# Two-layer graph network on one core: wide one-hot products, a reordered front, and W's low part on GpSimd

## Chip, cores and metric

One core of one Trainium2 chip runs one launch. The metric is device microseconds of that core, the median of several executions; lower is better. Engines are called as in the profile: PE (TensorE matmuls), PEld (its weight loads), DVE (VectorE), ACT (ScalarE), POOL (GpSimd), SP (the queue that issues loads).

## What is computed

1250 nodes with 512 features, 21250 edges. Cut to what matters here:

```python
h = relu(layernorm(x))
hw = h @ W + b_w                          # 512 x 512
e = leaky_relu((hw @ a[:512])[dst] + (hw @ a[512:])[src] + b_a)
w = exp(e)
x = x + segment_sum(w / denom[dst] * hw[src], dst)
h = relu(layernorm(x))
x = x + experts(h, edges)                 # 4 experts of 2 SAGE layers, top 2
```

## The kernel before

The edges become a dense matrix of counts, `CT[s, d]` = how many edges go from node s to node d. Nodes stand in T = 10 tiles of 125, edges in 170 chunks of 125. Attention is then a dense product over tiles, and both expert layers use the counts too. Everything after the first 103 us (attention, mean aggregation, experts) is not touched by the change.

**Hot stage** (`hot_block`, `hot_columns`). PE makes, for 8 chunks at a time, the one-hot rows of the edges' sources: two products of 500 columns (L1811) of `e_q` (edge numbers, their squares and a row of ones) with `q_sel`. A chunk's value is 1 where the number fits and at most 0 elsewhere, so an eviction with a maximum against 0 gives the one-hots `onehot_p`. There are 22 blocks (the last holds 2 chunks) in three pairs of banks, so block u waits for the eviction of block u-3. ACT evicts 21 blocks (L794), DVE one (`HOT_DVE`, L1189). Into PE's sequence four small steps are written by hand at fixed places: `spread_spans` (L1818) and `turn_edges` (L1824) wait for DVE's edge numbers, `sum_tables` (L1830) and `turn_tables` (L1840) for DVE's table of which chunks each window of 25 nodes needs.

**Tiles** (`tile_and_batch`). For each of the 10 tiles PE turns the normalized rows `h_f` (L1898), makes 25 count products for 5 windows (L1860; DVE makes their other operand `onehot_g`, L1301, 25 instructions a tile), the attention scores (L1879, L1882: `hT` times `wa`, where `wa` = W times the vectors a, made once by DVE in `sources`, L1184 to L1266), and 12 products of 512 columns with W (L1923 to L1925). Float32 values are split in a high part (rounded, fp32r) and a low part, `hT_hi`/`hT_lo` and `W0_hi`/`W0_lo`; three of the four partial products are taken. ACT makes high parts (L770), DVE low ones (L1285 for hT, L1270 for W).

Each engine works through its own program in order; waits on semaphores are the only link. DVE's order at the front: edge numbers, `x_stats` (statistics of the rows of x, L1195) in gaps, the table (L1202 to L1236), the last five statistics and `x_mv` (L1242), then tile 0: 25 one-hots, `scales` (L1249), `sources`, `hT_lo`, `W0_lo`, and then tile 1's one-hots. ACT's order: `q_sel`'s second half (L778), the square (L788), 21 evictions with `e_gc`, `column` (L804, the window's numbers that DVE's one-hots need) and `std` between them, then `h_f` (L811), `W0_hi`, `hT_hi`. POOL makes constants up to 10.4 us and is then idle until the tiles end.

The stationary `e_q` and moving `q_sel` have 65 rows: 32 numbers, 32 squares, 1 row of ones:

```python
e_q = at("e_q", [2 * CR + 1, CG, P], F32R, 15040)          # CR = 32
q_sel = at("q_sel", [2 * CR + 1, CR, P], F32R, R1 + 20480)
link(g.memset(f32(e_q[2 * CR:, :, :]), 1.0))
```

Of the kernel before, what the change touches and what calls it, by code (L numbers as in the profile page):

```python
# [37 lines left out]
def gnn_kernel(nc, x, src, dst, W0, b_w, a_vec, b_a, gate_W, gate_b, Wl, bl, Wr, out):  # L38
# [3 lines left out]
    P = 125  # L42
# [34 lines left out]
    with ctx:  # L77
# [65 lines left out]
        e_q = at("e_q", [2 * CR + 1, CG, P], F32R, 15040)  # L143
# [6 lines left out]
        q_row = at("q_row", [2 * CR + 1, P], F32, 21920)  # L150
        q_at = at("q_at", [2 * CR + 1, CR], F32, 22432)
        q_sel = at("q_sel", [2 * CR + 1, CR, P], F32R, R1 + 20480)
# [327 lines left out]
        HOT_DVE = (2,)  # L480
# [125 lines left out]
        def _(pool):  # L606
# [14 lines left out]
            link(g.memset(q_at[2 * CR:, :], 1.0))  # L621
# [26 lines left out]
            g.memset(tab_b[:], 0).then_inc(consts.sem, 1)  # L648
            beyond = counts_beyond(pool)
# [116 lines left out]
        def _(act):  # L766
# [83 lines left out]
            act.wait_ge(*norm_ready(1))  # L850
            norm(0)
            act.wait_ge(*w0_in(16))
            copy(W0_hi[:], W0_f[:]).then_inc(w0_hi_ready.sem, 1)

            for b in range(T):
# [12 lines left out]
                bias_in(b)  # L868
# [269 lines left out]
        def _(dve):  # L1138
# [14 lines left out]
            v.memset(q_row[CR:2 * CR, :], -1.0)  # L1153
            link(v.tensor_tensor(q_f[2 * CR:, :], q_f[2 * CR:, :], q_f[2 * CR:, :], ALU.mult))
            link(v.tensor_scalar(q_row[2 * CR:, :], q_f[2 * CR:, :], -1.0, 1.0, ALU.mult, ALU.add))
            dve.sem_inc(row_made.sem, 1)
            dve.wait_ge(*q_consts(2))
            for k in range(2):
                c = slice(8 * k, 8 * k + 8)
                v.tensor_tensor(q_sel[:, c, :], q_row[:].unsqueeze(1).broadcast_to([2 * CR + 1, 8, P]),  # L1160
                                q_at[:, c].unsqueeze(2).broadcast_to([2 * CR + 1, 8, P]), ALU.mult
# [30 lines left out]

            def row_stats(tiles):
# [4 lines left out]
            dve.wait_ge(*x_in(32))  # L1198
            row_stats(range(0, 2))
# [19 lines left out]
            row_stats(range(2, 4))  # L1219
            dve.wait_ge(*n_summed(1))  # L1220
            v.tensor_copy(tab_f[:, 2:3], ps[0:NW, 7, 0:1]).then_inc(tab_f_ready.sem, 1)
            row_stats(range(4, T // 2))
# [30 lines left out]
            def sources():  # L1253
# [4 lines left out]
                for w in range(2):  # L1258
                    dve.wait_ge(*wa_f_ready(2 * KC - 1 + w))
                    v.scalar_tensor_tensor(spill[w][0:P, :], bw_b[:], 1.0, a_b[0:P, w, :], ALU.mult, ALU.mult,  # L1260
                                           accum_out=ab[:, w:w + 1]).then_inc(ab_ready.sem, 1)
                dve.wait_ge(*wa_f_ready(2 * KC))
                link(v.tensor_copy(wa[:, :, 0:2], wa_f[:]))
                v.tensor_tensor(wa[:, :, 2:4], wa_f[:], f32(wa[:, :, 0:2]), ALU.subtract).then_inc(wa_ready.sem, 1)
                dve.wait_ge(*ab_ready(2))
                v.tensor_scalar(s_add[:], ab[:, 0:1], ab[:, 1:2], ba_c[:], ALU.add, ALU.add).then_inc(wa_ready.sem, 1)  # L1266

            def first_weights_low():
                dve.wait_ge(*w0_hi_ready(1))
                v.tensor_tensor(W0_lo[:], W0_f[:], f32(W0_hi[:]), ALU.subtract).then_inc(w0_lo_ready.sem, 1)  # L1270
# [992 lines left out]
```

## Time and profile before

| | us |
|---|---|
| median of 3 runs | 745.5 (745.43 to 745.51) |
| the profiled execution | 744.08 |
| its span | 742.3 |
| PE busy in the span | 717.8 (97%) |
| DVE, ACT, POOL busy | 428.0, 398.1, 184.1 |

The span is the stretch between the first and the last instruction; the execution has 1.8 us around it. In the rows, a line with "xN" holds N instructions: the first number is the start of the first, the second the time from it to the end of the last. Brackets give idle time before it and what ended it. Matmuls overlap, so each one's own duration is longer than the distance between two starts.

### The profile page before, as it was taken

How to read it: one execution, taken by the hardware profiler on the slowest of the kernel's cores; microseconds unless marked ns; L12 is line 12 of the kernel's file. 1: busy time of each engine (PE TensorE's matmuls, PEld its weight loads, DVE VectorE, ACT ScalarE, POOL GpSimd, SP SyncE). 2: the span in 40 equal slices, each digit the busy share in tenths (PEclk: the TensorE clock that was granted, in tenths of full speed). 3: DMA queues.
4: the chain of work that ended last, by engine and by line, in shares of the span. 5: the costliest groups of instructions: out<-in, count | busy, mean ns of one | idle time of the engine just before them, and what ended most of it. 6: DMA issues, size and time to landing. Idle time of an engine off the chain costs nothing.

```text
span 742.3 us, 12047 instructions
## 1 busy us (share of the span) xinstructions
PE 717.8 (97%) x3574; PEld 582.2 (78%) x3574; DVE 428.0 (58%) x1056; ACT 398.1 (54%) x897; POOL 184.1 (25%) x204
## 2 busy tenths in 40 slices
PE   5899999999999999999999999999999999999994
PEld 3589977888888888777777777878888888888883
DVE  8899889999752538622722622657444544444341
ACT  6966769677653521511511511347677667767751
POOL 4000000000000100850300010045666555655511
PEclk9999999999999999999999999999999999999998
DMA  9100000111501247799699695379844994438950
GB/s 207 39 4 3 4 3 18 53 35 35 165 8 58 79 123 240 217 333 326 228 354 328 200 359 197 99 184 264 300 93 88 264 343 120 86 69 225 290 156 6
DMA packets 46444, 115.19 MB, mean 155 GB/s; under 512 B 8340, under 2 KB 8552, under 8 KB 46361
## 3 DMA queue, kind: packets, MB, share of 16 engines
q1 hardware_dynamic: 28581, 77.60, 32.7%
q0 software_dynamic: 9136, 19.65, 11.6%
q10 hardware_dynamic: 8644, 16.86, 6.9%
q8 instruction: 48, 0.79, 0.4%
q14 instruction: 35, 0.29, 0.1%
HBM read 64.89 MB, written 50.08 MB: 155 GB/s over the span
## 4 chain that ended last, share of the span: by engine, by line
PE 92%; DVE 4%; ACT 1%; issue 1%; POOL 0%; DVEq 0%; ACTq 0%; POOLq 0%
PE ps L1783 16%; PE ps L1784 16%; PE ps L1785 16%; PE ps L2185 7%; PE ps L2184 6%; PE ps L2052 3%; PE ps L2053 3%; PE ps L1985 3%; PE ps L1860 3%; PE ps L1979 3%; PE ps L1980 3%; PE ps L2115 2%; PE ps L1923 1%; PE ps L1811 1%; PE ps L1925 1%; PE ps L1924 1%
## 5 line engine op out<-in xcount | busy, mean ns | idle before, releaser
L1110 ACT ACTIVATE agn<-ps,rec 32x128 f32<-32x128 f32 x336 | 120.7, 359 | 38.7 <-PE ps L2185 34.8
L1044 ACT ACTIVATE slots<-he_t 125x512 fp32r<-125x512 f32 x40 | 25.3, 635 | 150.9 <-DVE he_t L1581 146.6
L2185 PE MATMUL ps<-slots,CTs 125*128 x230 | 89.9, 391 | 0.0
L1581 DVE TENSOR_TENSOR he_t<-ps,b_b 125x512 f32<-125x512 f32 x40 | 27.6, 691 | 105.5 <-PE ps L1785 72.3
L728 POOL DMA_INDIRECT hrow<-t_d,piece_i x80 | 76.1, 951 | 25.7 <-issue 23.5
L2184 PE MATMUL ps<-slots,CTs 125*128 x207 | 80.7, 390 | 0.0
L1746 DVE TENSOR_TENSOR tm<-ps,b_b 128x512 f32<-128x512 f32 x23 | 15.9, 692 | 84.3 <-PE ps L1785 84.2
L1783 PE MATMUL ps<-W,agT_hi 128*125 128x512 f32 x160 | 63.5, 397 | 0.0
L1783 PE MATMUL ps<-W,h2T_hi 128*125 128x512 f32 x160 | 63.4, 396 | 0.0
L1785 PE MATMUL ps<-W,agT_lo 128*125 128x512 f32 x160 | 63.3, 396 | 0.0
L1784 PE MATMUL ps<-W,agT_hi 128*125 128x512 f32 x160 | 63.2, 395 | 0.0
L1784 PE MATMUL ps<-W,h2T_hi 128*125 128x512 f32 x160 | 63.2, 395 | 0.0
L1785 PE MATMUL ps<-W,h2T_lo 128*125 128x512 f32 x160 | 63.1, 394 | 0.0
L733 POOL DMA_INDIRECT out<-tg,rec x23 | 37.0, 1607 | 84.2 <-ACT tg L1099 64.3
L1674 DVE CAST CTs<-ps 125x512 fp32r<-125x512 f16 (+1 forms) x69 | 37.3, 596 | 29.1 <-PE ps L2115 29.1
L1301 DVE TENSOR_SCALAR onehot_g<-iota_h,column 125x250 bf16<-125x250 f16 x250 | 49.7, 282 | 5.9 <-PE ps L1860 4.6
L2185 PEld LDWEIGHTS ps<-slots,CTs 125*128 125x128 f32 x230 | 43.2, 188 | 9.7 <-issue 0.3
L2184 PEld LDWEIGHTS ps<-slots,CTs 125*128 125x128 f32 x207 | 38.9, 188 | 8.2
L1979 PE MATMUL ps<-nat_hi,p_hi 125*125 125x512 f32 x100 | 41.0, 410 | 0.2 <-issue 0.2
L712 POOL DMA_INDIRECT crow<-c_d,rec x23 | 22.7, 988 | 73.4 <-DVE W L1549 66.7
L1783 PE MATMUL ps<-slots,heT 128*128 x92 | 38.2, 415 | 1.7 <-DVE heT L1708 1.7
L1980 PE MATMUL ps<-nat_lo,p_hi 125*125 125x512 f32 x100 | 39.5, 395 | 0.0
(316 smaller groups left out, 1665.4 us busy)
## 6 DMA issues: line engine op xcount, KB each, us to landing
he_d<-slots SPq DMA_DIRECT2D x30, 448.0 KB
slots<-he_d SPq DMA_DIRECT2D x30, 448.0 KB
w_d<-slots SPq DMA_DIRECT2D x3, 4096.0 KB, 18.7
slots<-w_d SPq DMA_DIRECT2D x24, 512.0 KB
t_d<-he_t SPq DMA_DIRECT2D x40, 224.0 KB
raw<-in_L_gnn_Wl ACTq DMA_DIRECT2D x4, 1024.0 KB, 7.2
raw<-in_L_gnn_Wr ACTq DMA_DIRECT2D x4, 1024.0 KB, 5.6
slots<-in_L_gnn_Wl ACTq DMA_DIRECT2D x4, 1024.0 KB, 10.0
```

The source lines that it names most:

```text
L728: g.indirect_dma_start(hrow[i % HB][:, q, :], None, t_d.rearrange("e p t (r f) -> (e p t r) f", r=RQ), bass.IndirectOffsetOnAxis(ap=piece_ ...
L733: g.indirect_dma_start(out, bass.IndirectOffsetOnAxis(ap=i32(rec[:, i, 2:3]), axis=0), tg[i % 3][:], None, bounds_check=N - 1, oob_is_err= ...
L1110: last = a.activation(agn[32 * r:32 * r + 32, q, :], ps[n, 3 + i % 2, 128 * r:128 * r + 128], ACT.Copy, scale=rec[n, i, 4:5])
L1301: last = v.tensor_scalar(onehot_g[:, k, j, :], iota_h[:], column[:, b % 2 * BW + k, j:j + 1], None, ALU.is_equal)
L1674: v.tensor_copy(CTs[:, 4 * r:4 * r + n, :], turned_counts(r, n)).then_inc(cts_ready.sem, 1)
L1783: mm(o, l_hi, r_hi, start=start, stop=False)
L1784: mm(o, l_hi, r_lo, start=False, stop=False)
L1785: return mm(o, l_lo, r_hi, start=False, stop=stop)
L1979: mm(o, p_hi[:, g % RA, m, n], nat_hi[:, s, :], start=s == 0, stop=False)
L1980: mm(o, p_hi[:, g % RA, m, n], nat_lo[:, s, :], start=False, stop=False)
L2184: mm(o, CTs[:, t, :], part(k, P, t * 1024, P), start=False, stop=False)
L2185: last = mm(o, CTs[:, t, :], part(k, P, t * 1024 + D, P), start=False, stop=t == T - 1)
```

## The change

- `e_q`, `q_sel`, `q_row` and `q_at` get 128 rows. Rows 65 to 127 of `e_q` are ones and of `q_sel` zeros, so the products keep their values.
- `wake`: 12 float32 products of 128 x 128 on PE before the first block. Nothing reads them.
- The four small steps stand one or two blocks later in PE's order. DVE evicts block 3 in place of block 2.
- On ACT `W0_hi`, the bias copy of tile 0 and `h_f` of tile 0 move in among the evictions, and `e_gc` and `column` stand 2 and 3 blocks later.
- On DVE the statistics are spread otherwise, the register loads of tile 0's flags move ahead of the wait for the last statistics, `scales` comes after the first 5 of tile 0's one-hots, `hT_lo` comes before `sources`, and in `sources` `wa` comes before the two sums over the bias (L1260). `W0_lo` leaves DVE for POOL.
- On PE tile 0's products with W come before its scores and are grouped by operand; the scores wait for `wa` alone. `hT_hi` and `nat_hi` (the high part of h @ W) get the waits that this needs.

```diff
-        e_q = at("e_q", [2 * CR + 1, CG, P], F32R, 15040)
+        e_q = at("e_q", [128, CG, P], F32R, 15040)
-        q_sel = at("q_sel", [2 * CR + 1, CR, P], F32R, R1 + 20480)
+        q_sel = at("q_sel", [128, CR, P], F32R, R1 + 20480)
-        HOT_DVE = (2,)
+        HOT_DVE = (3,)
...
 (POOL)
+            pool.wait_ge(*w0_in(16))
+            pool.wait_ge(*w0_hi_ready(1))
+            g.tensor_tensor(W0_lo[:], W0_f[:], f32(W0_hi[:]), ALU.subtract).then_inc(w0_lo_ready.sem, 1)
...
 (ACT)
             def product_high(t):
                 act.wait_ge(*hw_done(t + 1))
+                if t == 0:
+                    act.wait_ge(*wa_ready(2))
...
             def turned_high0(b):
+                if b == 1:
+                    act.wait_ge(*s_done(1))
...
             for u in range(NU):
                 if u in HOT_ACT:
                     hot_columns(u)
-                if u == 3:
+                if u == 5:
                     act.wait_ge(*rows_turned(1))
                     copy(e_gc[:], ps[0:P, 7, 0:CG * CR]).then_inc(cols_ready.sem, 1)
-                if u == 10:
+                if u == 13:
                     act.wait_ge(*tab_ready(1))
                     columns(0)
+                if u == 15:
+                    act.wait_ge(*w0_in(16))
+                    copy(W0_hi[:], W0_f[:]).then_inc(w0_hi_ready.sem, 1)
...
+                if u == 17:
+                    bias_in(0)
+                if u == 18:
+                    act.wait_ge(*norm_ready(1))
+                    norm(0)
-            act.wait_ge(*norm_ready(1))
-            norm(0)
-            act.wait_ge(*w0_in(16))
-            copy(W0_hi[:], W0_f[:]).then_inc(w0_hi_ready.sem, 1)
...
 (DVE)
+            v.memset(q_row[2 * CR:, :], 0.0)
...
-            dve.wait_ge(*x_in(32))
-            row_stats(range(0, 2))
             hot_columns(HOT_DVE[0])
...
+            row_stats(range(2, T // 2))
             dve.wait_ge(*x_late_in(32))
-            link(row_stats(range(T // 2, T)))
+            late = row_stats(range(T // 2, T))
+            dve.wait_ge(*flag_ready(2))
+            dve.wait_ge(*tab_ready(1))
+            first_flags = batch_flags(0)
+            link(late)
...
+                    if b == 0 and k == 0:
+                        scales()
...
                 if b > 0:
                     product_low(b - 1)
-                else:
-                    scales()
-                    sources()
                 if b < T - 1:
                     turned_low0(b)
                 if b == 0:
-                    first_weights_low()
+                    sources()
...
 (PE)
+            def wake():
+                pe.wait_ge(*consts(2))
+                for _ in range(12):
+                    mm(ps[:, 7, 0:128], ones[:], ident[:], start=True, stop=True)
+
+            wake()
             for u in range(NU):
                 hot_block(u)
-                if u == 2:
+                if u == 3:
                     spread_spans()
-                if u == 3:
+                if u == 4:
                     turn_edges()
-                if u == 7:
+                if u == 9:
                     sum_tables()
-                if u == 8:
+                if u == 10:
                     turn_tables()
...
+                if b == 0:
+                    pe.wait_ge(*hT_hi_ready(1))
+                    for c in range(KC):
+                        first = mm(o, hT_hi[:, c], W0_hi[:, c], start=False, stop=False, skip_group_check=True)
+                        if c == 0:
+                            first.then_inc(batch_done.sem, 1)
+                    pe.wait_ge(*hT_lo_ready(1))
+                    for c in range(KC):
+                        mm(o, hT_lo[:, c], W0_hi[:, c], start=False, stop=False, skip_group_check=True)
+                    pe.wait_ge(*w0_lo_ready(1))
+                    for c in range(KC):
+                        last = mm(o, hT_hi[:, c], W0_lo[:, c], start=False, stop=c == KC - 1, skip_group_check=True)
+                    last.then_inc(hw_done.sem, 1)
+                    scores(0)
+                    return
```

ACT's program from the evictions after `column` of tile 0 to `hT_hi` of tile 0. Before (L794 evicts a block, L849 is `std`, `W_hi` is W0_hi):

```order
L794 ACTIVATE onehot_p<-ps 125x1000 x6
L849 ACTIVATE std<-std 125x10
L794 ACTIVATE onehot_p<-ps 125x1000 x4
L794 ACTIVATE onehot_p<-ps 125x250
L811 ACTIVATE h_f<-xs,shift,rstd 125x512
L770 ACTIVATE W_hi<-W_f 128x2048
L770 ACTIVATE hT_hi<-ps 128x500
```

And with the change:

```order
L798 ACTIVATE onehot_p<-ps 125x1000 x2
L774 ACTIVATE W_hi<-W_f 128x2048
L798 ACTIVATE onehot_p<-ps 125x1000
L860 ACTIVATE std<-std 125x10
L798 ACTIVATE onehot_p<-ps 125x1000
L774 ACTIVATE ps<-bw_b 125x512
L798 ACTIVATE onehot_p<-ps 125x1000
L815 ACTIVATE h_f<-xs,shift,rstd 125x512
L798 ACTIVATE onehot_p<-ps 125x1000 x2
L798 ACTIVATE onehot_p<-ps 125x250
L774 ACTIVATE hT_hi<-ps 128x500
```

Three instructions (`W_hi`, the bias into `ps`, `h_f`) now stand ahead of the last eviction, and nothing stands between it and `hT_hi`.

DVE's program in tile 0, after its one-hots. Before (the last 5 rows of `sources`, then hT's and W's low parts):

```order
L1260 SCALAR_TENSOR_TENSOR spill_94,ab<-bw_b,a_b 125x512
L1263 CAST wa<-wa_f 128x4x2
L1264 TENSOR_TENSOR wa<-wa_f,wa 128x4x2
L1266 TENSOR_SCALAR s_add<-ab,ba_c 125x1
L1285 TENSOR_TENSOR hT_lo<-ps,hT_hi 128x500
L1270 TENSOR_TENSOR W_lo<-W_f,W_hi 128x2048
```

And with the change, from the one-hots on (`sources` starts with the last row):

```order
L1317 TENSOR_SCALAR onehot_g<-iota_h,column 125x250 x5
L1271 RECIPROCAL rstd<-std 125x10
L1272 SCALAR_TENSOR_TENSOR shift<-x_mv,rstd 125x10
L1317 TENSOR_SCALAR onehot_g<-iota_h,column 125x250 x20
L1302 TENSOR_TENSOR hT_lo<-ps,hT_hi 128x500
L1198 SCALAR_TENSOR_TENSOR spill_93,wa_f<-W_f,a_b 128x512
```

`hT_lo` stands ahead of all of `sources` where it stood behind it, and `W_lo` is gone from DVE.

## Rows read from the trace of the kernel before

**Rows 1.** The page: busy time, and the chain that ended last.
```profile
PE 717.8 (97%) x3574; PEld 582.2 (78%) x3574; DVE 428.0 (58%) x1056; ACT 398.1 (54%) x897; POOL 184.1 (25%) x204
...
PE 92%; DVE 4%; ACT 1%; issue 1%; POOL 0%; DVEq 0%; ACTq 0%; POOLq 0%
```
**Rows 2.** Busy time by stage: stretch, its length, then each engine.
```profile
9.00:36.00 27.00, 24.30 (x61) 14.68 (x62) 22.62 (x86) 21.09 (x30) 1.31 (x6) 1.00 0.45 111
...
46.00:101.00 55.00, 55.00 (x399) 50.05 (x398) 50.39 (x224) 37.49 (x113) 0.00 (x0) 1.00 0.02 4
```
**Rows 3.** Timeline of PE, 9 to 36 us.
```profile
9.00 2.86 PE L1811 MATMUL ps<-q_sel,e_q 65*125 65x500 f32 x6 [9.00 <-ACT e_q L788]
11.80 1.51 PE L1818 MATMUL ps<-e_dg,ones 32*50 32x384 f32 x2
...
14.37 1.47 PE L1824 MATMUL ps<-ident,e_g 32*125 32x32 f32 x6
...
22.78 3.54 PE L1811 MATMUL ps<-q_sel,e_q 65*125 65x500 f32 x8
```
**Rows 4.** The chain in order of time: counts of tile 1, then one product with W (start, length).
```profile
46.43 2.71 PE ps L1860 x25
...
50.39 0.23 PE ps L1924
```
**Rows 5.** Timeline of PE, tile 0's transposes and counts.
```profile
35.93 1.07 PE L1898 MATMUL ps<-ident,h_f 125*128 125x125 f32 x4 [2.27 <-ACT h_f L811]
36.79 4.93 PE L1860 MATMUL ps<-onehot_g,onehot_p 125*125 125x250 bf16 x25
```
**Rows 6.** Timeline of ACT, hot stage and tile 0.
```profile
10.24 1.90 ACT L794 ACTIVATE onehot_p<-ps 125x1000 bf16<-125x1000 f32 x2 [1.28 <-PE ps L1811]
...
25.69 5.45 ACT L794 ACTIVATE onehot_p<-ps 125x1000 bf16<-125x1000 f32 x6
...
31.09 3.99 ACT L794 ACTIVATE onehot_p<-ps 125x1000 bf16<-125x1000 f32 x5
34.89 0.90 ACT L811 ACTIVATE h_f<-xs,shift,rstd 125x512 f32<-125x512 f32 x1
35.59 2.00 ACT L770 ACTIVATE W_hi<-W_f 128x2048 fp32r<-128x2048 f32 x1
37.39 0.67 ACT L770 ACTIVATE hT_hi<-ps 128x500 fp32r<-128x500 f32 x1
...
39.68 0.58 ACT L770 ACTIVATE ps<-bw_b 125x512 f32<-125x512 f32 x1
```
**Rows 7.** Groups of ACT, 0 to 46 us: count | busy, mean ns | idle before, released by.
```profile
L794 ACT ACTIVATE onehot_p<-ps 125x1000 bf16<-125x1000 f32 x20 | 18.7, 1018 | 5.6 <-PE ps L1811 5.6
...
L770 ACT ACTIVATE e_gc<-ps 125x192 f32<-125x192 f32 x1 | 0.3, 331 | 0.4 <-PE ps L1824 0.4
```
**Rows 8.** Timeline of DVE, from the spans to the one-hots of tile 1.
```profile
10.55 0.55 DVE L1173 TENSOR_TENSOR e_dg<-ident,e_mm 32x384 f32<-32x384 f32 x1 [0.76 <-POOL tab_b L648]
11.03 0.92 DVE L1176 SCALAR_TENSOR_TENSOR e_g<-e_g,e_t 32x750 f32<-32x750 f32 x1
...
28.23 4.96 DVE L1301 TENSOR_SCALAR onehot_g<-iota_h,column 125x250 bf16<-125x250 f16 x25 [1.33 <-issue]
...
33.44 0.69 DVE L1184 SCALAR_TENSOR_TENSOR spill<-W_f,a_b 128x512 f32<-128x512 f32 x1
...
40.03 0.67 DVE L1285 TENSOR_TENSOR hT_lo<-ps,hT_hi 128x500 fp32r<-128x500 f32 x1
40.62 2.28 DVE L1270 TENSOR_TENSOR W_lo<-W_f,W_hi 128x2048 fp32r<-128x2048 f32 x1
42.82 4.96 DVE L1301 TENSOR_SCALAR onehot_g<-iota_h,column 125x250 bf16<-125x250 f16 x25
```
**Rows 9.** Timeline of POOL, two of its constants.
```profile
2.87 0.21 POOL L627 MEMSET ones<- 128x128 f32 x1
...
9.34 0.39 POOL L644 CAST iota_h<-iota_i 125x250 f16<-125x250 int32 x1
```

More of the change, by code:

```diff
@@ L149, in gnn_kernel @@
         q_f = at("q_f", [2 * CR + 1, P], F32, 21408)
-        q_row = at("q_row", [2 * CR + 1, P], F32, 21920)
-        q_at = at("q_at", [2 * CR + 1, CR], F32, 22432)
-        q_sel = at("q_sel", [2 * CR + 1, CR, P], F32R, R1 + 20480)
+        q_row = at("q_row", [128, P], F32, 21920)
+        q_at = at("q_at", [128, CR], F32, 22432)
+        q_sel = at("q_sel", [128, CR, P], F32R, R1 + 20480)
         a_b = at("a_b", [128, 2, D], F32, R1)
@@ L620, in _ @@
                                      base=-CR * k, pattern=[[-1, CR]], channel_multiplier=1))
-            link(g.memset(q_at[2 * CR:, :], 1.0))
+            link(g.memset(q_at[2 * CR:2 * CR + 1, :], 1.0))
             pool.sem_inc(q_consts.sem, 1)
@@ L867, in _ @@
                     a.activation(spark[:], spark[:], ACT.Exp)
-                bias_in(b)
+                if b > 0:
+                    bias_in(b)
                 if b < T - 1:
@@ L1159, in _ @@
                 c = slice(8 * k, 8 * k + 8)
-                v.tensor_tensor(q_sel[:, c, :], q_row[:].unsqueeze(1).broadcast_to([2 * CR + 1, 8, P]),
-                                q_at[:, c].unsqueeze(2).broadcast_to([2 * CR + 1, 8, P]), ALU.mult
+                v.tensor_tensor(q_sel[:, c, :], q_row[:].unsqueeze(1).broadcast_to([128, 8, P]),
+                                q_at[:, c].unsqueeze(2).broadcast_to([128, 8, P]), ALU.mult
                                 ).then_inc(sel_ready.sem, 1)
@@ L1191, in hot_columns, with batch_flags @@
                                 ).then_inc(hot_dve_ready.sem, 1)
+            def batch_flags(b):
+                more = more_here(dve, b)
+                return more, dve.value_load(tab_b[0:1, b:b + 1, BW + 1:BW + 2], min_val=0, max_val=NW * NG)
             def row_stats(tiles):
@@ L1218, in _ @@
             v.tensor_scalar(tab_f[:, 1:2], tab_f[:, 1:2], -1.0, None, ALU.add).then_inc(n_ready.sem, 1)
-            row_stats(range(2, 4))
+            dve.wait_ge(*x_in(32))
+            row_stats(range(0, 1))
             dve.wait_ge(*n_summed(1))
             v.tensor_copy(tab_f[:, 2:3], ps[0:NW, 7, 0:1]).then_inc(tab_f_ready.sem, 1)
-            row_stats(range(4, T // 2))
+            row_stats(range(1, 2))
             dve.wait_ge(*tab_turned(1))
@@ L1257, in sources @@
                 source_vectors(1)
[L1258 to L1261, printed above, removed]
                 dve.wait_ge(*wa_f_ready(2 * KC))
@@ L1264, in sources @@
                 v.tensor_tensor(wa[:, :, 2:4], wa_f[:], f32(wa[:, :, 0:2]), ALU.subtract).then_inc(wa_ready.sem, 1)
+                for w in range(2):
+                    v.scalar_tensor_tensor(spill[w][0:P, :], bw_b[:], 1.0, a_b[0:P, w, :], ALU.mult, ALU.mult,
+                                           accum_out=ab[:, w:w + 1]).then_inc(ab_ready.sem, 1)
                 dve.wait_ge(*ab_ready(2))
                 v.tensor_scalar(s_add[:], ab[:, 0:1], ab[:, 1:2], ba_c[:], ALU.add, ALU.add).then_inc(wa_ready.sem, 1)
-            def first_weights_low():
-                dve.wait_ge(*w0_hi_ready(1))
-                v.tensor_tensor(W0_lo[:], W0_f[:], f32(W0_hi[:]), ALU.subtract).then_inc(w0_lo_ready.sem, 1)
             def one_hots(slot, w, first):
@@ L1288, in tile_and_batch @@
             def tile_and_batch(b):
-                more = more_here(dve, b)
-                before = dve.value_load(tab_b[0:1, b:b + 1, BW + 1:BW + 2], min_val=0, max_val=NW * NG)
+                more, before = batch_flags(b) if b > 0 else first_flags
                 dve.wait_ge(*column_ready(b + 1))
@@ L1876, in scores @@
                 if b == 0:
-                    pe.wait_ge(*wa_ready(2))
+                    pe.wait_ge(*wa_ready(1))
                 for c in range(KC):
                     first = mm(o, hT_hi[:, c], wa[:, c], start=c == 0, stop=False, skip_group_check=True)
-                    if c == 0:
+                    if c == 0 and b > 0:
                         first.then_inc(batch_done.sem, 1)
@@ L1916, in tile_and_batch @@
                     spread(0)
-                scores(b)
-                if b == 0:
-                    pe.wait_ge(*w0_lo_ready(1))
+                if b > 0:
+                    scores(b)
                 pe.wait_ge(*bias_ready(b + 1))
                 o = ps[0:P, 6, :]
+                if b == 0:
[13 more added lines that the diff above has]
+                    return
                 for c in range(KC):
```

5 lines of the change are left out of this document (2 added, 3 removed).

## The prediction

> **What bounds the kernel now.** I read the page first [rows 1]: PE is busy 97% of the span and the chain that ended last is PE for 92%, so elsewhere nothing but less PE work or fewer PE waits can count, and the change touches neither after 103 us. Then I read the stages [rows 2]. In the tile stage (46 to 101 us) PE is busy 55.00 of 55.00 us while DVE has 50.39: PE is the bound, and whatever the front gains or loses until PE is saturated is carried to the end one for one. So the question is when PE enters that stage. For this I follow DVE, since PE gets there only behind DVE [rows 8]: one-hots of tile 0 at 28.23, `sources` from 33.44, hT_lo at 40.03, W_lo at 40.62, tile 1's one-hots at 42.82, then tile 1's hT_lo. With that PE does tile 1's scores and products, then tile 2, and waits no more. **The start of tile 1's one-hots on DVE, 42.82 us, is the number that I move.**
>
> The front's other limit is the speed of PE. In the hot stage eight products of 500 columns take 3.54 us [rows 3]. Less 0.62 us, the time that one takes by itself, that is 2.92 for seven starts, 0.417 us each or 1.20 columns a ns. Products of 512 columns with W start every 0.23 us later on [rows 4], 2.2 a ns. So the front runs at the lower of the clock's two levels, 1.2 GHz, though the clock column of the stages says 1.00; up to about 41 us it can't be taken at its word. The 25 counts of tile 0 take 4.93 us against 2.71 in tile 1 [rows 4, 5], so the clock rises near their end. What PE did before it rose: transposes and counts with 125 rows, without a gap. What did not raise it: the hot stage's products with 65 rows, though PE was busy for 24.30 of its 27 us [rows 2]. That is the case for wide products.
>
> **The change, part by part.**
>
> *Wide rows.* The number of columns decides the time of a product, so the products themselves cost nothing. The 128-row operands lengthen no free dimension; one more small memset on DVE adds 0.1 us before the first block, covered only if the edges' load ends that late. I count +0.1.
>
> *wake.* It can start behind `ones` (2.87 + 0.21, [rows 9]), at about 3.2. A float32 product goes through PE in several passes: L1818, one product of 384 columns in two instructions, takes 1.51 us [rows 3], some 1.3 without the end, 3.4 ns a column. So 12 of 128 columns need 12 x 0.43 = 5.1 us, to 8.4; PE's first block starts at 9.00. Hidden with 0.6 us to spare.
>
> *ACT, first eviction.* 10.24 now [rows 6]. With PE at the upper level, the two products of block 0 end some 0.5 earlier; with the 0.1 above, 9.8: **-0.4**.
>
> *ACT, waits.* Between its first eviction and the last, ACT waits 5.6 + 0.4 less the 1.28 ahead of the first, 4.7 us [rows 6, 7], all for PE. An eviction takes ACT 0.89 us in a row ((5.45 - 1.00) / 5), a block takes PE 0.83 at the lower level and about 0.43 at the upper. So now each small step on PE (1.51 for L1818, 1.47 for L1824) hits ACT; then PE is ahead by two blocks, and only the first two steps, at half their time and with spans and edges that DVE has ready at 11.1 and 12.0 [rows 8], should still cost 0.2 each. **-4.3**.
>
> *ACT, what moves in.* `W_hi` 1.80 (35.59 to 37.39), h_f 0.70 (34.89 to 35.59), the bias 0.5 (0.58 alone) [rows 6]: **+3.0**. Block 3 for block 2 on DVE: 0. The last eviction so ends at 35.08 - 0.4 - 4.3 + 3.0 = 33.4, where 35.08 is 31.09 + 3.99.
>
> *Tile 0.* h_f is long done, W_hi too. In tile 1 the time from the start of the transposes to hT_hi is 0.7, and I take as much: PE 33.5, hT_hi 34.2 to 34.8, hT_lo on DVE 34.85, `sources` at 35.45. It takes 33.44 to 40.03 = 6.59, as now. Tile 1's one-hots then start at 42.05 in place of 42.82: **-0.8**. DVE's own front has slack: two statistics no longer stand ahead of its table, it waits less for PE, the 1.33 us of issue [rows 8] goes under the statistics, and its one-hots (28.23 to 33.19 now) end near 32 even with a wait for `std`, which comes behind W_hi. POOL's W_lo (next) is needed only after counts and eight products, near 38. The scores of tile 0 wait for `wa` at about 41; PE then stands still for some 2 us, which cost nothing, as tile 1's counts wait for DVE's one-hots anyway.
>
> *W_lo on POOL.* It leaves DVE (2.28 us, of which 2.20 were on the path; that gain is already in the 42.05, as are the 2 us that DVE now waits for hT_hi). No row shows a two-input operation on POOL. The bounds: 1.56 ns an element for a cast (0.39 for 250, [rows 9]) give 3.2 us for 2048, twice that for two inputs 6.4. I take 4.8, the middle: a cast is the nearest row, but has one input. W_hi ends at about 27.1 (six evictions, one of them small, `std`, the bias and h_f, 6.2 us in all, come between it and the end at 33.4), so 27.1 to 31.9, hidden by 4 us at least.
> The Trainium skill (GPSIMD Engine Reference, Elementwise: side-by-side cycle accounting) gives 4497 ns for a float32 tensor_tensor of 2048 on GpSimd and 2293 ns on DVE; this trace has 2.28 for DVE. By it W_lo would end at 31.6 and the sum would stay as it is.
>
> Sum: 745.5 - 0.8 = **744.7** us for the median (the profiled execution, 744.08 with a span of 742.3, would go to 743.3 and 741.5; its median stands 1.4 above it, and the shift is the same). What a measurement of this kernel can tell from no change is about 0.2%, 1.5 us.
>
> **Rivals.**
>
> *The clock stays down (slower).* If the 128 rows don't raise it, or it falls again at once, the moved work is still in ACT's stream: 35.08 + 3.0 = 38.1, transposes 1.1 with hT_hi at 39.3, `sources` at 40.5, one-hots at 47.1: +4.3, **749.8**. It decides where the first eviction and the waits together give less than 3.9 of the 5.1 us that they could. For it: no row shows fp32r products raising the clock, and once ACT is the bound PE is busy only half of the time at the upper level. Against it: wake is as long as the 125-row counts under which it rose [rows 5], and has 128 rows. If it falls back late, ACT paces all the same (0.83 against 0.89), and only the steps cost: 745 to 747.
>
> *POOL and DVE get in each other's way.* On POOL W_lo reads SBUF for 3.2 to 6.4 us from 27.1, exactly under the last 20 one-hots of tile 0. If DVE stood still for that long, they would end at 31.9 + 3.95 = 35.9 and hT_lo would wait for them: +1.05 over my sum, **745.7**; with 6.4 us it is 747.3, with 3.2 nothing. POOL stands idle from 10.4 us on in the trace of before, so that no row says yes or no; a one-hot takes 0.20 for 250 elements, which is more than one element a ns.
> The Trainium skill (SBUF: State Buffer, Who interferes with whom) says that DVE in a two-port mode and GpSimd lock each other out for a whole instruction. By that rule this case would be the likely one.
>
> *More than I count (faster).* ACT's waits vanish wholly (0.4), the small steps and hT_hi are quicker (0.3), the memset is covered (0.1): one-hots at 41.2, **743.9**.
>
> **Chances.** My forecast 0.55, of which it comes out beyond 1.5 us of gain 0.22 (the third rival with it); POOL and DVE 0.2, mostly within 0.2%; clock down or falling back 0.25, of which 0.2 slower by more than 1.5. So faster 0.24, same 0.53, slower 0.23. The range goes from 743.5, a little past the third rival, to 747.6, past POOL's dear end and the clock that falls back; it leaves out the clock that stays down.
>
> **What the profile of the changed kernel would show.** The products of 500 columns start 0.21 us apart, from the first block on; if 0.417, the first rival. ACT's waits for PE in the stage under 1 us, and its last eviction ends near 33.4. DVE's one-hots of tile 0 keep their 0.20 while W_lo runs; if there is a hole of several us, the second rival. W_lo on POOL takes 3.2 to 6.4. Tile 1's one-hots start near 42.0, and PE is saturated from 50 us on. I am wrong if that start moves by another amount, or if it moves so and the end does not follow.

## The result, and the profile of the changed kernel

The changed kernel takes **749.18 us** (median of 11, 748.37 to 756.18) against 745.5 (median of 11 in the same set, 745.38 to 746.92); ratio of time after to time before 1.0069, 95% interval 1.0054 to 1.0084 (intervals stand in brackets behind each ratio from here on). On a second chip, shared by one set of runs, it took 747.16 against 744.05: 1.0044 (1.0030 to 1.0057). I forecast 744.7 within 743.5 to 747.6. It is slower, and outside my range.

The profiled execution took 748.37 with a span of 746.6 (before: 744.08 and 742.3). The page's slices of the clock, and the two stages with the columns of [rows 2]:

```profile
PEclk9789999999999999999999999999999999999998
```
```profile
9.00:36.00 27.00, 18.21 (x65) 9.61 (x66) 23.56 (x77) 22.86 (x31) 5.90 (x8) 0.83 0.45 111
46.00:101.00 55.00, 53.76 (x378) 48.91 (x379) 50.39 (x224) 35.96 (x109) 0.00 (x0) 0.97 0.01 4
```

PE is busy for 6.1 us less in the hot stage (24.30 before). But PE is no longer full from 46 us on. The timeline of PE, which answers to [rows 3] and [rows 5]:

```profile
9.01 1.63 PE L1825 MATMUL ps<-q_sel,e_q 128*125 128x500 f32 x6 [1.34 <-ACT e_q L792]
...
11.54 0.84 PE L1832 MATMUL ps<-e_dg,ones 32*50 32x384 f32 x2
...
28.31 2.19 PE L1825 MATMUL ps<-q_sel,e_q 128*125 128x500 f32 x4 [1.97 <-ACT onehot_p L798]
...
35.03 1.09 PE L1918 MATMUL ps<-ident,h_f 125*128 125x125 f32 x4 [3.75 <-ACT onehot_p L798]
35.92 5.12 PE L1880 MATMUL ps<-onehot_g,onehot_p 125*125 125x250 bf16 x25
...
47.16 4.80 PE L1880 MATMUL ps<-onehot_g,onehot_p 125*125 125x250 bf16 x25 [2.06 <-DVE onehot_g L1317]
...
52.93 0.48 PE L1957 MATMUL ps<-W_hi,hT_hi 128*125 128x512 f32 x1
```

Six products in 1.63 us instead of 2.86 are the upper level, from the first block. At 28.31 ACT has kept PE waiting for 1.97 us (it was making W_hi), and the transposes at 35.03 with counts of 5.12 us are the lower level again. The timeline of ACT, which answers to [rows 6]:

```profile
9.77 2.79 ACT L798 ACTIVATE onehot_p<-ps 125x1000 bf16<-125x1000 f32 x3 [0.81 <-PE ps L1825]
...
25.37 2.00 ACT L774 ACTIVATE W_hi<-W_f 128x2048 fp32r<-128x2048 f32 x1
...
32.11 0.81 ACT L815 ACTIVATE h_f<-xs,shift,rstd 125x512 f32<-125x512 f32 x1 [1.45 <-DVE shift L1272]
32.83 2.15 ACT L798 ACTIVATE onehot_p<-ps 125x1000 bf16<-125x1000 f32 x3
36.16 0.59 ACT L774 ACTIVATE hT_hi<-ps 128x500 fp32r<-128x500 f32 x1 [1.18 <-PE ps L1918]
```

The timelines of DVE, which answers to [rows 8], and of POOL, which has no row before:

```profile
28.39 0.22 DVE L1271 RECIPROCAL rstd<-std 125x10 f32<-125x10 f32 x1 [1.41 <-ACT std L860]
28.64 3.44 DVE L1272 SCALAR_TENSOR_TENSOR shift<-x_mv,rstd 125x10 f32<-125x10 f32 x1
32.00 3.98 DVE L1317 TENSOR_SCALAR onehot_g<-iota_h,column 125x250 bf16<-125x250 f16 x20
36.78 0.68 DVE L1302 TENSOR_TENSOR hT_lo<-ps,hT_hi 128x500 fp32r<-128x500 f32 x1 [0.80 <-ACT hT_hi L774]
...
44.02 0.27 DVE L1287 TENSOR_SCALAR s_add<-ab,ba_c 125x1 f32<-125x1 f32 x1
```
```profile
45.83 1.26 DVE L1317 TENSOR_SCALAR onehot_g<-iota_h,column 125x250 bf16<-125x250 f16 x6 [1.54 <-issue]
```
```profile
27.52 4.53 POOL L652 TENSOR_TENSOR W_lo<-W_f,W_hi 128x2048 fp32r<-128x2048 f32 x1 [17.02 <-ACT W_hi L774]
```

Two things stand out. `shift`, 10 numbers a partition and 0.17 us of work, takes **3.44 us**: it ends as W_lo on POOL ends (32.05). And behind `s_add` DVE waits **1.54 us** for its own issue before tile 1's one-hots. These start at 45.83 instead of 42.82 [rows 8]: +3.0, where I had -0.8. Tile 1's products start at 52.93, 7.10 us after them.

The loss is then carried on. Two DVE instructions far behind, first before, then after:

```profile
481.62 0.69 DVE L1581 TENSOR_TENSOR he_t<-ps,b_b 125x512 f32<-125x512 f32 x1 [0.59 <-PE ps L1785]
491.79 0.69 DVE L1731 TENSOR_TENSOR aggT<-ps,aggT 128x512 fp32r<-128x512 f32 x1 [3.70 <-ACT aggT L770]
```
```profile
484.47 0.69 DVE L1595 TENSOR_TENSOR he_t<-ps,b_b 125x512 f32<-125x512 f32 x1 [0.59 <-PE ps L1799]
496.06 0.69 DVE L1745 TENSOR_TENSOR aggT<-ps,aggT 128x512 fp32r<-128x512 f32 x1 [5.12 <-ACT aggT L774]
```

At 481 us everything comes 2.85 later than before, ten microseconds on 4.27. The 1.42 between them arise in one place. PE turns the first means (`agn`) and ACT copies them; first the kernel before, then the changed one (PE, then ACT):

```profile
490.52 0.60 PE L2195 MATMUL ps<-ident,agn 128*128 128x128 f32 x4
491.16 0.60 ACT L770 ACTIVATE aggT<-ps 128x512 fp32r<-128x512 f32 x1 [4.22 <-PE ps L2195]
```
```profile
493.31 0.60 PE L2229 MATMUL ps<-ident,agn 128*128 128x128 f32 x4
495.43 0.60 ACT L774 ACTIVATE aggT<-ps 128x512 fp32r<-128x512 f32 x1 [5.64 <-remote]
```

ACT's program waits there for those four transposes alone, yet it starts 2.12 us after the first of them instead of 0.64; "remote" is a releaser that the profile does not know. What holds ACT is open. The profiled execution of the kernel before lies 1.4 under its median of 745.5, so most of its executions may hold the same delay, but no trace shows one. The front thus accounts for 2.9 of the 3.7 us.

### The profile page after: what moved, and what is told of

The parts are those of the page before. It is cut to its first block, busy times and chain, and to the rows that moved or that the text cites. A ratio compares the mean times of both kernels' runs of the same rounds, so it can differ in the third digit from the quotient of the medians.

```text
span 746.6 us, 12098 instructions
## 1 busy us (share of the span) xinstructions
PE 717.4 (96%) x3598; PEld 582.2 (78%) x3598; DVE 429.3 (57%) x1056; ACT 398.7 (53%) x897; POOL 188.1 (25%) x205
## 4 chain that ended last, share of the span: by engine, by line
PE 89%; ACT 4%; DVE 4%; issue 1%; another core or an unknown queue 1%; POOL 0%; ACTq 0%; DVEq 0%; POOLq 0%
PE ps L1797 16%; PE ps L1798 16%; PE ps L1799 16%; PE ps L2219 7%; PE ps L2218 6%; PE ps L2086 3%; PE ps L2087 3%; PE ps L2019 3%; PE ps L2013 3%; PE ps L2014 3%; PE ps L1880 3%; ACT onehot_p L798 2%; PE ps L2149 2%; PE ps L1957 1%; PE ps L1959 1%
```

## Experiments

**1. W_lo back on DVE.** POOL's three lines go; the same subtraction stands ahead of `turned_low0(0)`.

```diff
-            g.tensor_tensor(W0_lo[:], W0_f[:], f32(W0_hi[:]), ALU.subtract).then_inc(w0_lo_ready.sem, 1)
...
+                if b == 0:
+                    dve.wait_ge(*w0_hi_ready(1))
+                    v.tensor_tensor(W0_lo[:], W0_f[:], f32(W0_hi[:]), ALU.subtract).then_inc(w0_lo_ready.sem, 1)
                 if b < T - 1:
                     turned_low0(b)
```

> The changed kernel with W's low part back on DVE, between tile 0's one-hots and hT_lo (DVE stood idle there for 0.8 us, and would for 2 more without the stall). Theory A (DVE and GpSimd lock each other out of SBUF; that cost 3.4 us on DVE's shift and, through it, 1.45 us on ACT): shift takes 0.2 us instead of 3.44, the last one-hot of tile 0 is done near 32.5 instead of 36, ACT's last eviction ends near 33.5 instead of 35.0, hT_lo of tile 0 starts near 35.2 instead of 36.8; time 746.5 to 747.5, 1.5 to 2 us less than the changed kernel's 748.4. Rival B (the time is lost by the clock that falls at 27 us and in the register loads of 1.54 us, and GpSimd is innocent): shift is still slow or the tile's one-hots start no more than 0.5 us earlier on tile 1, time 748.4 or, with W_lo's 2.2 us on DVE's path, up to 750.

Measured: 745.43 us (745.25 to 746.20), 1.0020 (1.0011 to 1.0029), on a chip where the kernel before takes 743.96. Its DVE timeline:

```profile
28.65 0.17 DVE L1269 SCALAR_TENSOR_TENSOR shift<-x_mv,rstd 125x10 f32<-125x10 f32 x1
28.73 3.98 DVE L1314 TENSOR_SCALAR onehot_g<-iota_h,column 125x250 bf16<-125x250 f16 x20
32.63 2.28 DVE L1325 TENSOR_TENSOR W_lo<-W_f,W_hi 128x2048 fp32r<-128x2048 f32 x1
35.23 0.68 DVE L1299 TENSOR_TENSOR hT_lo<-ps,hT_hi 128x500 fp32r<-128x500 f32 x1 [0.32 <-ACT hT_hi L771]
...
44.28 2.82 DVE L1314 TENSOR_SCALAR onehot_g<-iota_h,column 125x250 bf16<-125x250 f16 x14 [1.53 <-issue]
```

`shift` is back at 0.17, h_f no longer waits, the last eviction ends at 33.43 (forecast: 33.4), and tile 1's one-hots start 1.55 earlier though DVE does 2.28 us more: that work fills time in which it waited for hT_hi. So theory A's mechanism is shown: with the GpSimd instruction gone, `shift` takes its own time again. Its time of 746.5 to 747.5 was meant for another chip; on one chip the two versions stand 1.4 us apart (12). The 1.53 of issue stay.

**2. W_lo on POOL alone**, in the kernel before: the converse.

```diff
+            pool.wait_ge(*w0_in(16))
+            pool.wait_ge(*w0_hi_ready(1))
+            g.tensor_tensor(W0_lo[:], W0_f[:], f32(W0_hi[:]), ALU.subtract).then_inc(w0_lo_ready.sem, 1)
...
-                    first_weights_low()
```

> The kernel before with one part of the change alone: W's low part on GpSimd, as soon as W_hi is there (at 37.6 us of the span). Theory A (GpSimd and VectorE keep each other from SBUF, whatever VectorE's instruction is): one of VectorE's instructions among the sources takes some 4.5 us more, hT_lo follows, the 2.28 us of W's low part are gone but 1.3 to 1.5 us of issue come open in their place; tile 1's one-hots begin 3.5 to 4 us later than 42.82, and the time is 747.4 to 748.0. Rival B (only many short instructions, such as the one-hots, are delayed): no instruction of the sources grows by over 1 us, tile 1's one-hots begin at 42.1 and the time is 744.8 or below.

750.64 us (750.28 to 751.52), 1.0070 (1.0056 to 1.0085). POOL, DVE and, from its timeline of PE, tile 0's first product with W:

```profile
37.74 5.05 POOL L651 TENSOR_TENSOR W_lo<-W_f,W_hi 128x2048 fp32r<-128x2048 f32 x1 [27.30 <-ACT W_hi L773]
```
```profile
37.72 0.69 DVE L1187 SCALAR_TENSOR_TENSOR spill<-W_f,a_b 128x512 f32<-128x512 f32 x1
...
38.34 5.00 DVE L1263 SCALAR_TENSOR_TENSOR spill<-bw_b,a_b 125x512 f32<-125x512 f32 x1
...
45.89 1.26 DVE L1300 TENSOR_SCALAR onehot_g<-iota_h,column 125x250 bf16<-125x250 f16 x6 [0.88 <-issue]
```
```profile
46.77 0.77 PE L1920 MATMUL ps<-W_hi,hT_hi 128*125 128x512 f32 x1
47.34 0.63 PE L1921 MATMUL ps<-W_lo,hT_hi 128*125 128x512 f32 x1
```

A source instruction grows from 0.69 to 5.00, and POOL's grows too (5.05 for 4.53), which fits that the one DVE had begun at 37.72 held it off for its 0.69: one case of the lock in the other direction. One-hots +3.07, as expected in kind. The time is 3 us above what I expected: tile 0's products now start 0.43 us apart instead of 0.23 [rows 4]. Between the end of tile 0's counts (41.6) and 46.8 PE had only the scores to do, and it comes back at the lower level.

**3. Rows back to 65**, the rest of the change as it is; `e_q`, `q_row` and `q_at` likewise.

```diff
-        q_sel = at("q_sel", [128, CR, P], F32R, R1 + 20480)
+        q_sel = at("q_sel", [2 * CR + 1, CR, P], F32R, R1 + 20480)
...
-            v.memset(q_row[2 * CR:, :], 0.0)
```

> The changed kernel with 65 rows again in the one-hot products, the wake products kept. Theory A (rows of the products decide whether the clock holds): the clock rises under the wake products near 6.5 us and falls again inside the hot stage, soon after 9 us; products of 500 columns start 0.417 us apart from there on, ACT waits over 3 us in the stage, time 750 to 753. Rival B (what counts is only that PE is busy): the clock is up until about 27 us as in the changed kernel, time 748.4.

750.11 us (749.29 to 751.19) against 743.96, 1.0077 (1.0061 to 1.0092). The first six products are as quick as the wide ones, then the granted clock falls to 0.50 (from 12 us on; in the changed kernel it is 1.00 from 9 to 25):

```profile
9.01 1.67 PE L1824 MATMUL ps<-q_sel,e_q 65*125 65x500 f32 x6 [0.46 <-ACT e_q L792]
...
15.43 4.60 PE L1824 MATMUL ps<-q_sel,e_q 65*125 65x500 f32 x10
```

Ten in 4.60 us are 0.42 apart. Tile 1's one-hots start at 49.30. Theory A holds.

**4. No `wake`.**

```diff
-            wake()
             for u in range(NU):
```

> The changed kernel without its 12 wake products. Theory A (wide products raise the clock by themselves, only later): products start 0.417 us apart until 13 to 17 us, then 0.23; ACT's first evictions and the two first small steps are late, last eviction 1 to 2 us later, time +1 to +2 over the changed kernel. Rival B (fp32r products don't raise it at all): 0.417 through the whole stage, last eviction near 39, time +3.5 to +4.5.

750.59 us (748.16 to 750.81) against 743.96, 1.0077 (1.0060 to 1.0093). PE's first eight products take 3.70 us, ten from 16.60 on 4.60, and only those from 21.39 on (two in 0.79) are quick; one-hots at 49.16. Wide products do raise the clock, but later than theory A's 13 to 17 us; `wake` raises it in time.

**5. Wide rows alone**, in the kernel before, twice; `e_q`, `q_row` and `q_at` likewise.

```diff
-        q_sel = at("q_sel", [2 * CR + 1, CR, P], F32R, R1 + 20480)
+        q_sel = at("q_sel", [128, CR, P], F32R, R1 + 20480)
...
+            v.memset(q_row[2 * CR:, :], 0.0)
```

> The kernel before with the 128 rows alone. Theory A (128 rows raise and hold the clock): spacing falls from 0.417 to 0.23 us near 13 to 17 us, ACT's waits fall from 4.7 to 2 to 3 us, tile 1's one-hots on DVE start 0.3 to 1 us earlier than 42.82 (DVE's own chain of 1.3 us of issue, one-hots and sources stays), time 744.5 to 745.3. Rival B (rows don't matter): spacing stays 0.417, time 745.5.

> The kernel before with the 128 rows alone, once more, to stand beside the others on one chip: ratio 0.9984 as in its first measurement if that was no accident of the chip (0.9975 to 0.9993); 1.000 or more if it was.

742.68 us (742.27 to 744.29) against 743.96: 0.9984 (0.9975 to 0.9993). The second time 745.16 (743.90 to 745.83) against 745.48: 0.9992 (0.9983 to 1.0001). It is the only part that gained, 0.1 to 0.2%, and only the first time beyond its interval. In the two profiles the clock rises at different places, and tile 1's one-hots start at 42.60 and 41.36.

**6. Wide rows and `wake`**, in the kernel before: as 5, and

```diff
+            wake()
             for u in range(NU):
```

> The kernel before with the 128 rows and the twelve products ahead of the first block. Theory A (the rows alone took it to 742.68, with the clock up only at 20.8 us; the products ahead raise it before the first block, as they did in the changed kernel): the clock is up from about 7 us to 25 us or more, the blocks' products are 0.23 us apart from the start, but ScalarE's copies set their pace: the last eviction ends within 0.5 us of the wide version's 34.02, and the time is 742.4 (742.0 to 742.9). Rival B (the early clock is paid back by an earlier fall: the transposes and counts of tile 0 then run at the low clock): 743 to 744.

745.54 us (743.16 to 752.87) against 745.40, 1.0022 (0.9999 to 1.0045): inconclusive by the times, which spread over 10 us, and neither theory's time. In its trace the last eviction ends at 33.01, a whole 1.0 earlier than in 5, and tile 1's one-hots start at 41.16, 1.7 before the kernel before.

**7. Flags early.** As 1, and DVE reads tile 1's table values beside tile 0's.

```diff
-            first_flags = batch_flags(0)
+            first_flags = [batch_flags(b) for b in range(2)]
```

> The changed kernel with W's low part on VectorE between tile 0's one-hots and hT_lo (that version took 745.43 us, its one-hots of tile 1 began at 44.28 us of the span, after 1.53 us of issue), and VectorE reads tile 1's two table values together with tile 0's, ahead of the last statistics. Theory A (those 1.5 us are register loads from the table, which nothing covers once W's low part has left the place behind the sources): the idle time before tile 1's one-hots falls from 1.53 us to under 0.6, they begin at 43.0 +- 0.4, and the time is 744.1 (743.7 to 744.5). Rival B (the 1.5 us are the skipped branch, not the loads): the idle time stays above 1.2 us and the time is 745.4. Rival C (TensorE's counts and not VectorE's one-hots set the pace behind tile 0): the one-hots begin earlier and the time stays at 745.4.

746.67 us (745.86 to 750.26) against 745.40, 1.0023 (1.0010 to 1.0035). Issue before the one-hots 0.59 us, their start 43.32. So 0.94 of the 1.53 were the register reads; whether the rest is the skipped branch was not tried. Theory A holds for the front, but not for the time: the ratio is that of experiment 1. Its trace takes on 1.44 us between 481 and 492 us, where that of experiment 1 did not.

**8. W_lo on DVE behind `s_add`**, as late as in the kernel before.

```diff
                 if b == 0:
                     sources()
+                    dve.wait_ge(*w0_hi_ready(1))
+                    v.tensor_tensor(W0_lo[:], W0_f[:], f32(W0_hi[:]), ALU.subtract).then_inc(w0_lo_ready.sem, 1)
```

> The changed kernel with W's low part on VectorE again, behind the sources and the scalar sum, where the kernel before has it. Theory A (2.28 us of work there cover the 1.53 us of issue that stand open otherwise): tile 1's one-hots begin 1.5 us sooner than in the version with W's low part ahead of hT_lo, at 42.8 +- 0.4, and the time is 744.0 (743.6 to 744.4), the same as with the early register reads. Rival B (TensorE now waits for W's low part, its product ends later by as much and the copy of tile 0's product with it): no gain, 745.4.

750.02 us (748.76 to 756.76), 1.0090 (1.0056 to 1.0123). Both theories fell, and the time is worse than either gave. The issue is covered (one-hots at 44.85 behind W_lo, no wait), but PE waits for W_lo:

```profile
44.99 1.60 PE L1951 MATMUL ps<-W_lo,hT_hi 128*125 128x512 f32 x4 [3.80 <-DVE W_lo L1328]
47.93 1.09 PE L1917 MATMUL ps<-ident,h_f 125*128 125x125 f32 x4
48.81 4.59 PE L1879 MATMUL ps<-onehot_g,onehot_p 125*125 125x250 bf16 x25
```

and then does tile 0's last products, the transposes and the counts at the lower level, so that tile 1's products start at 54.04.

**9. TensorE kept busy.** As 7, with products that nobody reads (bank 7, columns 256 to 383).

```diff
+            def fill(n):
+                for _ in range(n):
+                    mm(ps[:, 7, 256:384], ones[:], ident[:], start=True, stop=True)
+
+            FILL = {16: 4, 18: 6, 21: 6}
...
+                if u == 14:
+                    pe.wait_ge(*tab_ready(1))
+                if u >= 14:
+                    fill(FILL.get(u, 1))
...
+                if b == 1:
+                    fill(6)
```

> The version with W's low part on VectorE and early register reads (tile 1's counts from 44.64 us of its span, 4.86 us for 25; without the early reads 45.60 and 4.79), with 21 further products of 128x128 on TensorE between blocks 14 and 21, most of them where it stood still, and 6 ahead of tile 1's counts; their results are read by nobody. Theory A (the granted clock falls at 24.7 and again at 45.2 us because TensorE stood still just before, and the second fall costs some 2 us in tile 1's counts): the clock stays high from 8 us on, tile 0's counts take 2.9 us instead of 4.8, tile 1's counts are paced by VectorE's one-hots (43.3 + 5) and end at 48.5 instead of 49.5, and the time is 1 us below that version: ratio to the kernel before 1.001 (1.000 to 1.002) after 1.0023. Rival B (the fall has nothing to do with what TensorE does in the gaps): the clock falls at the same places, the extra products cost up to 1 us, ratio 1.0023 to 1.004. Rival C (the clock stays, but the time is set elsewhere): tile 1's counts end at 48.5 and the ratio stays at 1.002.

747.11 us (745.51 to 749.76) against 745.48, 1.0022 (1.0010 to 1.0034): no gain. Two stretches of the changed kernel, then of this one (columns as in [rows 2], the clock is the third number from the end):

```profile
27.00:40.00 13.00, 7.73 (x29) 6.24 (x30) 10.77 (x32) 8.88 (x17) 4.53 (x1) 0.50 0.01 2
...
47.00:51.00 4.00, 3.85 (x19) 3.47 (x20) 4.00 (x21) 0.61 (x1) 0.00 (x0) 0.57 0.02 6
```
```profile
27.00:40.00 13.00, 10.58 (x68) 8.76 (x67) 11.56 (x40) 10.32 (x22) 0.00 (x0) 1.00 0.01 2
...
47.00:51.00 4.00, 3.65 (x24) 2.98 (x24) 4.00 (x18) 1.72 (x6) 0.00 (x0) 1.00 0.02 6
```

The clock does stay up when PE is kept busy. Yet:

```profile
44.70 4.78 PE L1889 MATMUL ps<-onehot_g,onehot_p 125*125 125x250 bf16 x25 [0.17 <-issue]
...
50.47 0.48 PE L1968 MATMUL ps<-W_hi,hT_hi 128*125 128x512 f32 x1
```

Tile 1's counts take 4.78 us at the upper level as at the lower: they wait for DVE's one-hots (43.38 on, 4.96 us), five by five, and the scores behind them for DVE's hT_lo. I had expected their end at 48.5; it is 49.5 as before. The low clock under them, in the changed kernel too, costs nothing.

**10. Another order on DVE**, otherwise as 7. **11.** The same with products as in 9, three in place of the last six.

```diff
-            def sources():
+            def first_sources():
                 dve.wait_ge(*w0_in(16))
                 dve.wait_ge(*small_in(48))
                 source_vectors(0)
+
+            def sources():
                 source_vectors(1)
...
-                    if b == 0 and k == 0:
+                    if b == 0 and k == 2:
                         scales()
...
+                if b == 0:
+                    first_sources()
                 if b < T - 1:
                     turned_low0(b)
```

> The same version without further products, in another order on VectorE: the reciprocal and the shifts behind the third group of tile 0's one-hots (it waited 1.41 us for std), and the first of the two source vectors ahead of hT_lo. Theory A (VectorE's own path is 2 us too long, TensorE's is the next): tile 1's one-hots begin at 41.3 instead of 43.32, and tile 1's counts are then set by TensorE, from 43.1 on; they end at 46.1 if the clock is high and at 48.0 if it is low, against 49.5: ratio 0.9985 to 1.001. Rival B (hT_lo, now 0.9 us later, holds up tile 0's product): one-hots at 41.3, counts of tile 1 not before 44.0, ratio 1.001 to 1.003.

> Both together (three further products ahead of tile 1's counts instead of six). Theory A: clock high from 8 us on, tile 0's counts 2.9 us, tile 1's one-hots from 41.3 and its counts from 41.6 to 46.4 us, 2.6 us before the kernel before (49.0): ratio 0.9965 (0.995 to 0.998), below that of the kernel before with wide rows alone (0.9984). Rival B (it is the clock or the order alone that counts): no better than the better of the two single versions.

10: 744.20 us (742.73 to 748.56) against 745.48, 0.9986 (0.9968 to 1.0003). 11: 745.64 (743.38 to 750.55), 0.9998 (0.9978 to 1.0019). One-hots start at 41.42 in both, 1.4 before the kernel before, and tile 1's products at 48.52 in both: DVE's path still sets it, not PE's as I had expected. Here the clock does cost, in 10 (first) but not in 11:

```profile
48.52 0.75 PE L1961 MATMUL ps<-W_hi,hT_hi 128*125 128x512 f32 x1
49.06 0.63 PE L1962 MATMUL ps<-W_lo,hT_hi 128*125 128x512 f32 x1
...
52.94 0.59 PE L1922 MATMUL ps<-ident,h_f 125*128 125x125 f32 x4
```
```profile
48.52 0.48 PE L1972 MATMUL ps<-W_hi,hT_hi 128*125 128x512 f32 x1
...
51.38 0.59 PE L1931 MATMUL ps<-ident,h_f 125*128 125x125 f32 x4
```

The twelve products take 4.42 us in 10, where the first eight start some 0.43 apart, and 2.86 in 11 at the upper level throughout: 1.56 us, on the path. No pause of PE stands ahead of the fall in 10: the granted clock is 1.00 from 44 to 48 us and 0.64 from 48 to 50, and since 33.5 us PE had never stood still for more than 0.2 us at a stretch. In 11, where the added products had kept the clock up from the start, it does not fall; why it falls in 10 is open. Theory A of 11 (a ratio of 0.9965) failed. Of 11's lead in the trace (1.47 us at 400 us) 0.1 is left at the end. No version beats the kernel before beyond its interval but the wide rows alone, in their first measurement.

**12. What wanders.** The changed kernel and experiment 1 again, on one chip, and the kernel before with W_lo computed twice:

```diff
+                link(v.tensor_tensor(W0_lo[:], W0_f[:], f32(W0_hi[:]), ALU.subtract))
                 v.tensor_tensor(W0_lo[:], W0_f[:], f32(W0_hi[:]), ALU.subtract).then_inc(w0_lo_ready.sem, 1)
```

> The changed kernel once more, beside the others on one chip. Its trace stands 2.9 us behind that of the kernel before from 160 to 480 us, yet its median is 3.7 us up and its executions reach from 748.4 to 756.2. Theory A (the changed front itself makes it wander): median 748.4 to 750, highest above 751. Rival B (that was the one chip): all executions within 1 us.

> The changed kernel with W's low part on VectorE once more, on the same chip as the changed kernel itself. Theory A (1.56 us of the front are GpSimd's lock on VectorE): 1.6 to 3.1 us below the changed kernel's median. Whether it wanders here (its first 11 executions lay within 1 us, on another chip) tells whether the wandering goes with GpSimd's part of the change (Theory A: it does not wander here either) or with the chip (Rival B: it wanders as widely as the changed kernel).

> The kernel before with W's low part computed twice on VectorE, one after the other: nothing of the change is in it, but everything behind tile 0 comes 2.3 us later (tile 1's one-hots at 45.1 instead of 42.82), by about as much as in the changed kernel. Theory A (a later front costs what it costs, and what lies behind 480 us adds nothing on the whole): 747.8 (747.4 to 748.5), executions as close together as those of the kernel before. Rival B (any shift of the front against what comes behind 480 us makes the executions wander): 747.8 or more, with single ones above 750. If TensorE, which then stands still for 2.3 us more, falls to the low clock in tile 1's product, 1.5 us come on top.

The changed kernel: 747.16 us (746.87 to 747.72). Experiment 1: 745.73 (745.37 to 746.35), 1.0022 (1.0013 to 1.0031). The kernel before: 744.05. So W_lo on POOL instead of DVE costs 1.4 us of 3.1 (a little less than the 1.6 expected), the rest is there without it, and executions up to 756 don't belong to the change as such: here its five lie within 1 us (rival B). The changed front repeats to 0.02 us (`shift` 3.43, one-hots at 45.85); what differs is behind 481 us:

```profile
484.49 0.69 DVE L1595 TENSOR_TENSOR he_t<-ps,b_b 125x512 f32<-125x512 f32 x1 [0.60 <-PE ps L1799]
494.55 0.69 DVE L1745 TENSOR_TENSOR aggT<-ps,aggT 128x512 fp32r<-128x512 f32 x1 [3.55 <-ACT aggT L774]
```

The same comparison for more traces, in us behind the trace of the kernel before (a minus is ahead of it):

| | tile 1's one-hots | `he_t` at 481 | `aggT` at 492 | whole execution |
|---|---|---|---|---|
| changed kernel | 3.01 | 2.85 | 4.27 | 4.29 |
| again | 3.03 | 2.87 | 2.76 | 2.79 |
| experiment 1 | 1.46 | 1.28 | 1.16 | 1.17 |
| 5, second | -1.46 | -1.52 | -0.10 | -0.10 |
| 7 | 0.50 | 0.34 | 1.78 | 1.78 |
| 9 | 0.56 | 0.38 | 1.09 | 3.74 |
| 11 | -1.40 | -1.47 | -0.09 | -0.08 |

Up to 481 us the start of tile 1's one-hots is carried on to within 0.2 us, a gain as well as a loss. At the copy shown in the section on the result up to 1.5 us are added, in some traces and not in others, and that takes back the whole gain of 5 and 11; in 9 another 2.65 come later.

`b_late`: 748.38 us (747.74 to 748.90), 1.0055 (1.0041 to 1.0069), in theory A's range. One-hots come 2.32 late (45.14), as I expected, but tile 0's products (12 from 45.28, 0.43 apart) run at the lower level after 2.74 us without work, and its trace is 4.8 behind. The kernel before thus loses 4.3 us by a delay of 2.3.

## Why the prediction was wrong, step by step

- **What bounds the kernel: right up to 481 us.** From tile 1's one-hots to tile 1's products it is 7.09 us in the kernel before, 7.10 in the changed one, 7.09 in experiments 7 and 9 and 7.10 in 10 and 11; their start is the number to move as long as tile 0's products run at the upper level. Where these fell (2 and `b_late`) it is 9.65 and 9.77, and in 8, where they also wait for W_lo, 9.19. "Carried to the end one for one" fails behind 481 us (table in 12): even the forecast's gain of 0.8 could have been lost there.
- **Wide rows, `wake`, first eviction, ACT's waits: right.** First eviction 9.77 (9.8). ACT's large evictions wait 1.7 us in all for PE, 0.81 of them ahead of the first: 0.9 between, where I had 0.4. With the lock away, the last eviction ends at 33.43 (33.4). With either part missing the kernel is 6.2 and 6.6 us above the kernel before (3, 4); the first rival had 4.3, without lock and issue.
- **W_lo on POOL "hidden by 4 us at least": the first step that failed.** The sum held nothing for POOL's effect on DVE, and it cost 1.6 us. "POOL and DVE get in each other's way" was the right rival, priced at the wrong instruction: I took the last 20 one-hots as its only victim, with 0 to +2.6 us (+1.05 at 4.8), and gave it 0.2. The victim was `shift`, for which ACT's h_f, and with it the last eviction and the transposes, wait: last eviction 34.98 for 33.4. The one-hots were merely queued behind it, so no run shows whether they would have stood still themselves. W_lo itself took 4.53 (4.8).
The Trainium skill (SBUF: State Buffer, Who interferes with whom) also names DVE instructions with two SBUF inputs, against a GpSimd instruction that reads SBUF, and clears those with one input outside the two-port modes; the prediction quoted only the part on two-port modes. The traces agree with these two: `shift` and, in 2, one instruction of `sources` have two inputs and took 3.44 and 5.00 us, and the reciprocal has one and took its 0.22 while W_lo ran.
- **"That gain is already in the 42.05": the second step that failed.** Taking W_lo from between hT_lo and tile 1's one-hots removed 2.20 us of work and uncovered 1.54 us of register reads and branch, which had gone under it. I had seen such an issue ahead of tile 0's one-hots [rows 8] and placed that one well, but did not ask where tile 1's was hidden.
- **Tile 0: 0.65 short.** hT_lo was at 36.78 for 34.85. 1.6 of that comes from the last eviction; the other 0.35 lies between it and hT_lo, where the transposes ran at the lower level; and from there to `s_add`'s end and the sources 0.3 more. Together 1.6 + 0.35 + 0.3 + 1.54 = 3.8, the distance from 42.05 to 45.83: instead of 0.8 sooner tile 1's one-hots start 3.0 later.
- **"PE then stands still for some 2 us, which cost nothing": right here** (2.06 us, and experiment 9), but by luck of what came next. A like pause (3.45 and 2.74 us) ahead of products that pace the kernel costs some 2.6 us in 2 and `b_late`; in 10 such products lost 1.56 us to the lower level without any pause.
- **The range.** It was built from the one-hots' delay alone; no term had a bound for work uncovered at DVE. Still open are 0.8 of the 3.7 us of the first measurement, and why executions of most front variants spread over several us on one chip and not on another.

## What to carry to other kernels

When an instruction leaves an engine, look for what ran under it: register reads and branches ahead of the next block cost 1.5 us here once their cover was gone. Before work goes to GpSimd, list every VectorE instruction in its shadow by its number of SBUF inputs, the tiny ones too, and price the lock at who waits for the first of them. A pause of TensorE is not free because nobody waits during it: read which work follows at the lower level, and whether that work sets the pace. And where a change moves the front by a microsecond, follow it through the trace to the end: here 1.4 us were lost or kept at one copy far behind.

## What the runs showed of the hardware

- A DVE instruction of 125x10 with two SBUF inputs stood 3.44 us behind a GpSimd tensor_tensor; a GpSimd one grew by 0.5 us when DVE had begun first.
- Products of 65 rows did not hold the upper level that `wake` had given, (3), though ACT made them wait no longer than in the changed kernel (0.26 and 0.28 us ahead of the seventh); with 128 rows it held to 27 us. One trace each.
- Two executions of one kernel can have the clock rise at different places: `b_wide` and its repetition have tile 1's one-hots 1.24 us apart.
- 2.3 us more work on DVE made the kernel before 4.3 us slower, through the clock.
